# Sorted expert groups with an area of rows for each expert, routed chunk by chunk

## What is computed

```python
x = x + 0.5 * _L0_ffn_ref(_layernorm(x), ...)      # group 0: 8 experts, top 2, swiglu
x = x + _L0_attn_ref(_layernorm(x), ...)           # self attention, top-k scores kept
x = x + 0.5 * _L0_ffn_ref(_layernorm(x), ...)      # group 1: the same experts again
x = x + 0.5 * _L1_ffn_ref(_layernorm(x), ...)      # group 2: 8 other experts, top 2, relu
x = x + _L1_attn_ref(_layernorm(x), ...)           # cross attention, 16 heads, 256 keys
x = x + 0.5 * _L1_ffn_ref(_layernorm(x), ...)      # group 3: those experts again

def _L1_ffn_ref(x, W1, b1, W2, b2, Wg, bg):
    gate_logits = xt @ Wg.T + bg
    w, idx = jax.lax.top_k(gate_logits, K)         # K = 2
    w = jax.nn.softmax(w, axis=1)
    h = jax.nn.relu(jnp.einsum('td,ehd->eth', xt, W1) + b1[:, None, :])
    y = jnp.einsum('eth,eoh->eto', h, W2) + b2[:, None, :]
    comb = (jax.nn.one_hot(idx, E) * w[..., None]).sum(axis=1)
    out = jnp.einsum('eto,te->to', y, comb)
```

## Time and profile before

| | us |
|---|---|
| median of 3 runs | 1110.07 |
| lowest, highest | 1108.25, 1110.55 |
| the profiled execution | 1111.54 |
| its span in the trace | 1109.7 |
| busy: PE, DVE, ACT, POOL | 964.8, 793.0, 551.2, 456.8 |

### The profile page before, as it was taken

How to read it: one execution, slowest core, us unless ns; L and a number is a source line. 1 busy time by engine, 2 the same in 40 slices (tenths; PEclk the granted TensorE clock), 3 DMA queues, 4 the chain that set the end, 5 groups by cost and what they waited for, 6 DMA issues and landing times.

```text
span 1109.7 us, 17763 instructions
## 1 busy us (share of the span) xinstructions
PE 964.8 (87%) x5108; PEld 734.7 (66%) x5108; DVE 793.0 (71%) x3045; ACT 551.2 (50%) x1242; POOL 456.8 (41%) x538
## 2 busy tenths in 40 slices
PE   5979967779989899867899888998999999995994
PEld 3559845667777677755697465795666666564973
DVE  6745598999999999996455774326878787873424
ACT  2337643444454444435775322457666676651541
POOL 2350078866666566657201715302521011135035
...
GB/s 312 185 133 191 139 20 217 40 1 1 0 1 1 1 1 1 1 105 37 114 253 203 92 40 51 158 235 37 34 11 1 1 2 1 1 91 93 240 161 71
DMA packets 59423, 90.90 MB, mean 82 GB/s; under 512 B 11056, under 2 KB 40896, under 8 KB 58944
## 3 DMA queue, kind: packets, MB, share of 16 engines
...
## 4 chain that ended last, share of the span: by engine, by line
PE 43%; DVE 28%; issue 4%; POOL 3%; ACT 2%; DMA 2%; POOLq 0%; ACTq 0%; DVEq 0%
DVE vb L1518 10%; PE bank L695 9%; DVE sg L1526 9%; PE bank L379 6%; PE bank L679 5%; PE bank L392 4%; PE bank L336 3%; PE bank L348 3%; PE bank L663 2%; PE bank L669 2%; DMA yg<-ys,posu 2%; POOL yg L1903 1%; PE bank L367 1%; PE bank L484 1%; DVE x L1382 1%
## 5 line engine op out<-in xcount | busy, mean ns | idle before, releaser
L1903 POOL DMA_INDIRECT yg<-ys,posu x96 | 95.0, 989 | 160.0 <-DMA ys<-ysb 88.4
L1550 POOL TENSOR_SCALAR vb<-sS,vb 128x256 f32<-128x256 f32 x126 | 115.7, 930 | 97.8 <-DVE vb L1518 92.5
L1518 DVE MAX8 vb<-sg 128x8 f32<-128x256 f32 x384 | 142.5, 412 | 0.0
L1889 POOL DMA_INDIRECT xs<-xnS,posu x96 | 95.1, 991 | 84.0 <-DVE posu L1350 49.1
L1013 ACT ACTIVATE hb<-sS,negm 128x256 f32<-128x256 f32 x128 | 58.0, 502 | 132.7 <-POOL negm L1919 132.7
L379 PE MATMUL bank<-xbT,ws 128*128 128x256 f32 x456 | 115.2, 390 | 0.1
L484 PEld LDWEIGHTS bank<-kn,qn 128*128 128x128 f32 x512 | 110.7, 317 | 0.0
L484 PE MATMUL bank<-kn,qn 128*128 128x17 f32 x512 | 104.8, 346 | 0.0
L1526 DVE MATCH_REPLACE8 sg<-vb,sg 128x256 f32<-128x256 f32 x256 | 102.6, 407 | 0.0
L470 PE MATMUL bank<-pk,hb 128*128 128x128 f32 x256 | 67.8, 418 | 36.5 <-POOL hb L1556 35.2
L336 PE MATMUL bank<-xnT,ws 128*128 128x512 f32 x192 | 96.4, 637 | 1.2 <-ACT VO L1138 0.9
...
## 6 DMA issues: line engine op xcount, KB each, us to landing
...
```

The lines of the kernel that those rows point to most:

```text
L1518: e.max(m8s[:, m:m + 8], s).then_inc(A["tk"], 1)
L1550: i = e.tensor_scalar(msk[:, n * S:n * S + S], sS[:, s:s + S], m[:, n, TOPK - 1:TOPK], None, ALU.is_ge)
L1889: e.indirect_dma_start(xs[:, :], at(g, t, k), xnS[:, g.tile(t)], None).then_inc(s_sc, 16)
L1903: e.indirect_dma_start(yg[:, y:y + D], None, ys[:, :], at(g, t, k)).then_inc(s_g[t % GY], 16)
```

## The change

Groups `S1`, `S2` and `S3` use a table of their own, `xsc`, of 55 x 256 rows, in which expert e's rows begin at 1536 e, so that the row of a token no longer depends on how many rows other experts get. What is left is how many rows the same expert had in earlier chunks, kept in `offs`. So each chunk is ranked by itself (`pe_rank_part`, 8 matmuls), placed by itself (`dve_place_part`, 5 instructions on DVE) and sent at once (8 scatters). When all three are placed, `dve_place_end` (20 instructions) makes `emap`, `rmap` (from which row of `xsc` a block is read) and `posg` (the rows of `ys` for the gathers). SP reads `rmap` by a `value_load` for each x block. The table is filled with zeros by five DMAs of 1.44 MB, which SP issues at the start of a0 behind the loads of `pk[3]` and `pk[4]`; `qn` is set to zero over 3840 columns in place of 2432. `S0` stays as it was.

```diff
+CAP = GT * P
+AREAS = E * CAP // BS + NBLK - 2 * GT * P // BS
...
-        NORM_A0 = {38: 0, 46: 1, 55: 2}
-        T_A0 = {41: 0, 49: 1, 56: 2}
-        LOGITS_A0 = {42: 0, 50: 1, 57: 2}
-        RANK_A0 = 58
+        NORM_A0 = {24: 0, 40: 1, 55: 2}
+        T_A0 = {25: 0, 41: 1, 56: 2}
+        LOGITS_A0 = {26: 0, 42: 1, 57: 2}
+        RANK_A0 = {32: 0, 48: 1, 58: 2}
+
+        SCATTER_A0 = {33 + n: n for n in range(8)}
+        SCATTER_A0 |= {49 + n: 8 + n for n in range(8)}
+        SCATTER_A0 |= {59 + n: 16 + n for n in range(5)}
...
-        STATS_A1 = {FB + 3: 0, 2 * FB + 3: 1, 3 * FB + 1: 2}
-        T_A1 = {FB + 4: 0, 2 * FB + 4: 1, 3 * FB + 1: 2}
-        LOGITS_A1 = {FB + 5: 0, 2 * FB + 5: 1, 3 * FB + 2: 2}
-        CHOICE_A1 = {FB + 6: 0, 2 * FB + 6: 1, 3 * FB + 2: 2}
-        END_A1 = {FB + 1: 0, 2 * FB + 1: 1, 3 * FB: 2}
-        LAST_LOGITS, RANK_A1 = 3 * FB + 2, 3 * FB + 3
-
-        COMBINE_A1 = {1: (0, 1), 2: (2, 3), 4: (4,), 5: (5,), 6: (6,), 7: (7,), 10: (8,), 13: (9,), 14: (10,), 15: (11,)}
+        END_A1 = {FB + 1: 0, 2 * FB + 1: 1, 3 * FB + 1: 2}
+        STATS_A1 = {FB + 4: 0, 2 * FB + 4: 1, 3 * FB + 2: 2}
+        T_A1 = {FB + 5: 0, 2 * FB + 5: 1, 3 * FB + 3: 2}
+        LOGITS_A1 = {FB + 6: 0, 2 * FB + 6: 1, 3 * FB + 4: 2}
+        CHOICE_A1 = {FB + 7: 0, 2 * FB + 7: 1, 3 * FB + 4: 2}
+        RANK_A1 = {2 * FB: 0, 3 * FB: 1, 3 * FB + 5: 2}
+        LAST_LOGITS = 3 * FB + 4
+
+        COMBINE_A1 = {1: (0, 1), 2: (2, 3), 4: (4,), 5: (5,), 6: (6,), 7: (7,), 9: (8,), 10: (9,), 14: (10,), 15: (11,)}
...
             pe_dense(e, D1, pe_beside_d1, 1)
             pe_a1_bv(e)
             pe_a1_VT(e, 0)
+            e.wait_ge(M["off"], S2.parts[1].nth)
+            pe_rank_part(e, S2.parts[2])
+            pe_a1_VT(e, 1)
+            e.wait_ge(M["off"], S2.off_done())
             pe_T(e, D2.m)
-            pe_a1_VT(e, 1)
-            pe_rank(e, S2)
             pe_a1_VT(e, 2)
...
             dve_a1_bv(e)
             dve_xn(e, D2.m)
             dve_a1_VT(e, 0)
+            dve_place_part(e, S2.parts[2])
             dve_a1_VT(e, 1)
-            dve_place(e, S2)
+            dve_place_end(e, S2)
             dve_a1_VT(e, 2)
...
             if p in STATS_A1:
                 dve_stats(e, S3.parts[STATS_A1[p]])
+            if p >= 0 and f == 3 and c + 1 < NC:
+                dve_a1_xn(e, c + 1)
+            if p in T_A1:
+                dve_xn(e, S3.parts[T_A1[p]])
             if p in COMBINE_A1:
                 dve_combine(e, S2, COMBINE_A1[p])
...
-            if p >= 0 and f == 3 and c + 1 < NC:
-                dve_a1_xn(e, c + 1)
-            if p in T_A1:
-                dve_xn(e, S3.parts[T_A1[p]])
...
-            if p == RANK_A1:
-                dve_place(e, S3)
+            if p in RANK_A1:
+                dve_place_part(e, S3.parts[RANK_A1[p]])
+            elif p - 1 in RANK_A1 and RANK_A1[p - 1] == 2:
+                dve_place_end(e, S3)
             if p >= 0:
                 dve_a1_acc(e, p, 2)
                 dve_a1_acc(e, p, 3)
...
             pool_rstd(e, S2.parts[2])
+            pool_scatter(e, S2, 0, 4 * CT)
             pool_rstd(e, D2.m)
-            pool_scatter(e, S2, beat=beat_values)
+            pool_scatter(e, S2, 4 * CT, beat=beat_values)
...
         def load_x_block(e, g, n):
             b = g.first + n
             after(e, M["bT"], b - XSLOTS + 1)
-            e.dma_start(xb[b % XSLOTS][:, :], xs[n * BS:(n + 1) * BS, :].rearrange("(p t) d -> p (t d)", p=P)).then_inc(s_xl[b % XSLOTS], 16)
+            rows = xs[n * BS:(n + 1) * BS, :]
+            if g.i:
+                rows = xsc[bass.ds(e.value_load(rmap[g.p][0:1, n:n + 1], min_val=0, max_val=(AREAS - 1) * BS), BS), :]
+            e.dma_start(xb[b % XSLOTS][:, :], rows.rearrange("(p t) d -> p (t d)", p=P)).then_inc(s_xl[b % XSLOTS], 16)
...
         def sync_blocks(e, g):
-            e.wait_ge(M["map"], g.i + 1)
+            e.wait_ge(M["map"], 2 * g.i + 1)
...
             e.dma_start(pk[4][:, :], packed[4]).then_inc(s_ld[4], 16)
+            for n in range(5):
+                e.dma_start(xsc[n * ZEROS:(n + 1) * ZEROS, :].rearrange("(p r) d -> p (r d)", p=P),
+                            qn[:, 4 * S:4 * S + ZEROS]).then_inc(s_fill, 16)
```

More of the change, by code:

```diff
@@ L126, in build @@
         posu = [sb(f"posu{n}", 2 * GT, U32) for n in range(2)]
+        offs, posg = sb("offs", 4 * E), [sb(f"posg{n}", 2 * GT, U32) for n in range(2)]
+        delta, bsum, gd = sb("delta", E), sb("bsum", NBLK), sb("gd", 2 * GT)
+        rmap = [sb(f"rmap{n}", NBLK, mybir.dt.int32) for n in range(2)]
         beyond, em = sb("beyond", NBLK * E), sb("em", NBLK)
@@ L199, in build, with __init__ @@
                        "stats2 mv2 end x bv bve VT VTe VO VOe VOo keep")
+        ZEROS = AREAS * BS // 5
         ORDER = (3, 0, 1, 2)
         class Part:
-            def __init__(self, q, stage, c, slot, T, logits=0, by_tanh=True):
+            def __init__(self, q, stage, c, slot, T, logits=0, by_tanh=True, rank=None):
                 self.q, self.stage, self.c, self.slot = q, stage, c, slot
                 self.T, self.logits, self.by_tanh = bank[T], bank[logits], by_tanh
+                self.rank = bank[logits if rank is None else rank]
                 self.glu = stage < 2
@@ L227, in __init__, with off_done, posg_done @@
                 self.xs = {0: E, 2: 3 * E, 3: 3 * E}.get(i)
-                for m in parts:
-                    m.g = self
+                self.rows = xsc if i else xs
+                self.place0 = 9 + PLACES * (i - 1) if i else 0
+                for n, m in enumerate(parts):
+                    m.g, m.n = self, n
+                    m.nth = 3 * i - 1 + n
+                    m.nth_posu = 4 * i - 2 + n
+            def off_done(self):
+                return 3 * self.i + 1
+            def posg_done(self):
+                return 4 * self.i + 1
             def tile(self, t):
@@ L305, in pe_rank, with pe_rank_part @@
                 i = e.matmul(b[:, GT * E:GT * E + E], ones16[:, :], O[:, t * E:t * E + E], start=t == 0, stop=t == GT - 1)
+            i.then_inc(M["rank"], 1)
+        def pe_rank_part(e, m):
+            b, lo = m.rank, m.slot * CT * E
+            e.wait_ge(R["O"], 3 * m.g.i + m.n + 1)
+            e.wait_ge(R["lg"], m.q + 1)
+            e.matmul(b[:, 0:CT * E], upto[:, :], O[:, lo:lo + CT * E], start=True, stop=False)
+            for t in range(1, CT):
+                e.matmul(b[:, t * E:CT * E], ones16[:, :], O[:, lo:lo + (CT - t) * E], start=False, stop=t == CT - 1)
+            for t in range(CT):
+                i = e.matmul(b[:, CT * E:CT * E + E], ones16[:, :], O[:, lo + t * E:lo + t * E + E], start=t == 0, stop=t == CT - 1)
             i.then_inc(M["rank"], 1)
@@ L1299, in dve_choice @@
                 e.wait_ge(R["ids"], 2 * m.q + 2)
-                after(e, M["rank"], m.g.i)
+                after(e, M["rank"], 1 if m.g is S1 else m.nth - 3)
                 e.tensor_tensor(m.of(O, E), m.of(eq, E, 0), m.of(eq, E, 1), ALU.add).then_inc(R["O"], 1)
@@ L1357, in dve_place, with dve_place_part @@
             e.tensor_scalar(emap[g.p][:, :], em[:, :], E - 1.0, float(P), ALU.min, ALU.mult).then_inc(M["map"], 1)
+        def dve_place_part(e, m):
+            g, b, done = m.g, m.rank, m.g.place0 + m.n * PLACE_PART
+            e.wait_ge(M["rank"], m.nth)
+            e.wait_ge(M["off"], m.nth - 1)
+            lo = offs[:, m.n * E:m.n * E + E]
+            e.tensor_tensor(three(pos[:, 0:CT * E], E), three(b[:, 0:CT * E], E), rows_of(lo, CT, E), ALU.add).then_inc(M["place"], 1)
+            e.tensor_tensor(offs[:, (m.n + 1) * E:(m.n + 2) * E], b[:, CT * E:CT * E + E], lo, ALU.add).then_inc(M["off"], 1)
+            e.wait_ge(M["place"], done + 1)
+            at_ = m.slot * CT * E
+            e.tensor_tensor(three(posk[:, 0:2 * CT * E], CT * E), three(eq[:, :], NT * E)[:, :, at_:at_ + CT * E],
+                            rows_of(pos[:, 0:CT * E], 2, CT * E), ALU.mult).then_inc(M["place"], 1)
+            e.wait_ge(M["place"], done + 2)
+            to = slice(m.slot * CT, m.slot * CT + CT)
+            e.tensor_reduce(three(posf[:, :], GT)[:, :, to], posk[:, 0:2 * CT * E].rearrange("p (j t e) -> p j t e", j=2, e=E),
+                            axis=mybir.AxisListType.X, op=ALU.add).then_inc(M["place"], 1)
+            e.wait_ge(M["place"], done + 3)
+            e.tensor_copy(three(posu[g.p][:, :], GT)[:, :, to], three(posf[:, :], GT)[:, :, to]).then_inc(M["posu"], 1)
@@ L2010, in gpsimd_program @@
             pool_a1_keep(e, 1)
[L2011 to L2018 removed]
+            pool_a1_end(e, 0)
+            pool_a1_rstd(e, 2)
+            pool_a1_keep(e, 2)
+            pool_rstd(e, S3.parts[0])
+            pool_a1_end(e, 1)
+            pool_scatter(e, S3, 0, 2 * CT)
+            pool_a1_rstd(e, 3)
+            pool_a1_keep(e, 3)
+            pool_rstd(e, S3.parts[1])
+            pool_a1_end(e, 2)
+            pool_rstd(e, S3.parts[2])
+            pool_scatter(e, S3, 2 * CT)
```

135 lines of the change are left out of this document (94 added, 41 removed).

## The result

The changed kernel takes 1125.1 us (median of 4 runs, 1124.63 to 1127.55), the kernel before 1110.31 (median of 4, 1108.25 to 1111.12): 1.0141 times as long, 95% interval 1.012 to 1.0161. The direction was right; the loss is 15 us, where 4 were forecast, and the time lies above the range.

A forecast was written before the change was run, and what follows sets the result against it. Limits were taken stage by stage: DVE in a0, the POOL-DVE path between D1 and D2, PE's wait at S3's start. Terms 0.2 + 4.2 + 2 + 5.8 + 1.0 - 9.9 + 0.8 = +4.1 on 1110.07 gave 1114.2 us, range 1107 to 1120.

The forecast's parts named there:

- the maps as S3's gate: Start of S3: `rmap`, not the scatters, holds back the weight loads; PE starts at 1010.9 us instead of 1020.83.
- pairs and start of S3: From the pairs to S3's first PE work: earlier normalizing, ranking and scatters save 9.9 us together.
- D2 starts +5.8 later: Between D1 and D2: POOL's 16 scatters make D2's 1/std 5.7 us late, so D2 starts 5.8 us later.
- Setup +0.2: Kernel start: one 8-column DVE instruction for `offs` costs 0.2 us; the larger `qn` memset hides before a POOL wait.
- The fill: In a0: writing 7.2 MB of zeros while DMA engines are full delays gathers, +2 us (0 to +5).
- R3: Rival, a0: the zero fill makes gathers wait, DVE's 3.94 us wait recurring for two more steps; 1119 us, chance 0.13.
- S2's blocks: Blocks of S2: SP's extra value read makes it slower than PE, mostly hidden by its lead; +1.0 us (0 to +2.5).
- The pairs: Pair steps up to step 30: normalizing first and routing spread out make step 30 begin 6.8 us earlier.
- R1: Rival, between D1 and D2: the late 1/std of D2 costs nothing; 1108.4 us, chance 0.17.
- R2: Rival, start of S3: the maps do not gate it, nothing else differs; 1111 us, chance 0.07.
- R4: Rival, blocks of S2 and S3: SP's rate bounds them without a lead, 7.6 us each; 1122 or more, chance 0.05.
- R5: Rival, start of S3: still behind its scatters, as POOL reaches the last 8 late; 1117 us, chance 0.04.

The follow-up runs named there:

- Experiments 5 and 6: Changed kernel with D2's 1/std ahead of 16 scatters and S2's `dve_place_end` behind VO's copies (both 1.0036, either alone 1.0058), or with 12 added PE matmuls (1.0142).
- e6_areas_s3: Kernel before with the change for S3 alone, S1 and S2 routed as before, zero fill from a0's 16th step: ratio 0.9939.
- experiment 5: Runs on one faster chip against the kernel before: changed kernel 1.0124, with 12 added PE matmuls 1.0142, with the two moves 1.0036.
- the two moves: Changed kernel with D2's 1/std ahead of the 16 scatters and S2's `dve_place_end` behind VO's four copies: ratio 1.0036 to the kernel before.
- e5_pe_fed: Changed kernel with 12 more 128x256 matmuls on PE between D1 and D2, results unread: ratio 1.0142 to the kernel before.

## Why the prediction was wrong

- **The direction and most mechanisms held**, at the sizes given. DVE's work in a0 (5.0 for 4.2), 1/std behind 16 scatters (6.4 for 5.8), the maps as S3's gate (`rmap` 8.0 us into step 30 for 8.2), pairs and start of S3 (-9.0 for -9.9), S3's blocks (0.8 for 0.8).
- **The step that failed** is the term "D2 starts +5.8 later". It priced the wait of PE by its length, and held the work behind it at its old durations. PE ran at 1.2 GHz through VO and D2's first matmuls: +3.7 between the two traces. The durations were taken from the one trace of before, in which VO had 2.4 GHz for three of four steps. Experiments 5 and 6 show that mending one wait is not enough, and one trace of four that mending both can bring the clock back. `e6_areas_s3` shows +3.8 in this stretch with no edit in it. So a part of the 3.7, and perhaps all, is luck of the trace of before, and what lowers the clock stays open. On the side of the waits: in all the runs on the chip of experiment 5 the two moves gave back 9.9 by medians, and by the landmarks of its traces 5.9 of it are waits.
- **"Setup +0.2"** was 1.9. The first matmul of D0 came 0.6 late, as in all 16 traces with this setup and in none of the three others: that part is the edit's, three times the forecast. At S0's start PE waited 4.86 us for its first x block where it was 3.31, and its clock rose later (the 1.3 behind that). With such a setup the other traces on the faster chips began a0 0.5 to 4.6 late, so most of the 1.9 is a spread of that place; the range should have held it. As none began early, and only one trace of before is from such a chip, a part of it may be the edit's too.
- **The fill** was 3.0 for 2, within its bounds, and R3 only in part: one long wait more, not two. In other traces it came as R3 has it, with two more waits (3.61 and 1.49 in `e5_pe_fed`) and a shift of up to +5.5.
- **S2's blocks** 1.6 for 1.0: the pitch of 2.38 was too high (2.20), but the lead too large in the sum.
- **The pairs** gave 6.2 for 6.8, for partly other reasons: the three boundaries gave more than their waits (0.9, 2.0 and 2.0, net of the routing steps moved behind them), a rank cost 0.4 and not 0.3, and the last five steps gave 2.1 and not 3.3.
- **R1 is refuted**: undone with the place's end, the 1/std gives back nearly 10 us. R2 is refuted by the maps, which were ready 8.0 us into step 30 and ahead of all weight loads. R4, SP without a lead, did not come; R5 neither. (R2's own sum comes to 1110.3 and not 1111, which bears on nothing else.)
- All six misses beyond 0.5 us fell on the side of a loss. Each bound of the range took in its own unknown, none the clock.
